# Edge scores of a graph attention layer: held scatters, a split slope and an adding gather

## The chip, the cores and the metric

The kernel runs on one core of a Trainium2 chip. The metric is the device time of one execution in microseconds, the median of the runs. Below, PE is TensorE, DVE is VectorE, ACT is ScalarE, POOL is GpSimd and SP is SyncE, which issues most DMAs here; ACTq and SPq are the instruction queues of ACT and SP.

## The reference

The program runs two layers over 1250 nodes with rows of 1024 numbers. Each layer is a graph part plus a linear attention, then a mixture of experts. The change touches the graph attention of the first layer:

```python
x = x * rsqrt(mean(x*x) + eps) * rms_w @ W_down      # 1250 x 256
xl = (x @ Wl).reshape(n, 4, 64);  xr = (x @ Wr).reshape(n, 4, 64)
msg = xl[src] + xr[dst]
act = where(msg > 0, msg, 0.2 * msg)
e = einsum('ehd,hd->eh', act, att)                   # a score for each edge and head
p = exp(e - segment_max(e, dst)[dst])
out = segment_sum(p / segment_sum(p, dst)[dst] * xl[src], dst) @ W_up
```

There are 20,000 edges in both directions plus one loop per node, 21,250 in all. The second layer also sums the rows of all sources of a node, so a table of how often an edge stands between two nodes is used twice.

## The kernel before

One core works through phases, one after the other; each phase is a block in which every engine has its own list of instructions, and all five meet at a barrier at its end. The core does not hold an edge list sorted by node. It writes the scores of all edges into a dense table `scores` in HBM (1250 x 1250 x 4 numbers, 25 MB), which is filled with -1e30 beforehand, and counts edges in a table `at`. The phases that matter:

- `norm_phase` (norm0, L116) normalizes `x`; ACT then issues 12 of the 40 tiles of the fill of `scores` (`Fill.issue`, L110, two DMAs each through `move_rows`, L35).
- `gat_project_phase` (L325): ACT issues the other 28 tiles first, then rounds the weights. PE computes `xl` and `xr`, which go to HBM, and DVE the scores of the loops (`loops`).
- `count_phase` (L548) sets up its tables (spans, node numbers), then for ten tiles of nodes DVE writes one-hot rows (`hot_d` L681, `hot_s` L683) that PE multiplies to counts (L755). ACT turns them round and SP stores them in `at`.
- `mix_phase` (mix0, L1063): linear attention in 8 slabs, bound to PE's matmuls. `output_phase` (out0, L1499) multiplies it with its weight.
- `gat_phase` (L768) reads `scores` and `at` tile by tile, takes the softmax and the weighted sum.

The edges ride along in three of them: they are cut in 85 batches of 250 edges (`EB` = 2 columns of 125). 18 batches are done in the count phase, 48 in mix0 (six per slab) and 19 in out0. For each batch POOL gathers the rows of `xl` and of `xr` with indirect DMAs (L478, two each), DVE computes the scores in `EdgeTurns.step` (L527: add L540, slope L541, times `att` L542, sum L543), and POOL scatters them into `scores` (L490, two). On POOL, `batch` (L483) waits for DVE's score of a batch, then issues scatter, gather, gather, scatter, gather, gather, where the gathers are for the batch two further on; each scatter waits until the one before it has landed (`s_sc`), since edges may repeat. The buffers have three slots (`RING`), and DVE copies the indices of each batch into a small tile (`columns`, L456). The diagonal is written by 11 small DMAs (L507) after the fill has landed.

Further on, `expert_phase` adds its rows into `x` with an indirect DMA that adds (L2136, 104 rows), and gathers with a plain one (L2123, 104 rows).

## Time and profile before

| what | value |
|---|---|
| median of 3 runs | 3541.19 us (3536.98 to 3546.23) |
| the profiled execution, own time | 3539.15 us |
| its span, first to last instruction | 3537.4 us |
| mean granted clock of PE | 0.871 |
| busy: PE, DVE, ACT, POOL | 77%, 46%, 25%, 26% |
| indirect DMAs issued by POOL for edges | 510 (170 scatters, 340 gathers) |

Times are microseconds from the span's start. An instruction of POOL that issues an indirect DMA is shown with the time in which POOL writes its descriptors; the transfer runs on behind it. In a line of a timeline the bracket tells how long the engine was idle before the instruction, and what ended that; "issue" means nothing that the profile can name. A wait for several semaphores is put down to the last one.

### The profile page before, as it was taken

The numbers are of one execution on the slowest core, as the hardware profiler recorded it, in microseconds if no ns is written. First come the engines' busy times: TensorE is split into PE (matmuls) and PEld (weight loads), VectorE is DVE, ScalarE is ACT, GpSimd is POOL, SyncE is SP. The second block draws the span as 40 slices with busy tenths as digits, with TensorE's granted clock in tenths as the row PEclk, the third lists the DMA queues.
The fourth block names the chain that finished last, engine by engine and source line by source line (L and its number), as shares of the span: only waits on it lengthen the run. The fifth ranks groups of instructions, "written<-read, shape, count | busy, mean of one in ns | idle before, by whom it ended". The sixth has DMA issues, their size and how long they took to land. (4 is left out here: it accounts for less than half of the span.)

```text
span 3537.4 us, 53669 instructions
## 1 busy us (share of the span) xinstructions
PE 2739.5 (77%) x19204; PEld 2520.8 (71%) x19204; DVE 1622.7 (46%) x3435; ACT 870.0 (25%) x1619; POOL 915.4 (26%) x790
## 2 busy tenths in 40 slices
PE   1267667887957659648995899899998979996458
PEld 1244457887847558637884899889997979996347
DVE  4078845554554359656554322223334422224445
ACT  3011023333211036313452101034442111101033
POOL 0036547677765612102221000000000000000054
PEclk6688888998978869857997899999998979998579
DMA  7722233333236398535874411111101553114064
GB/s 187 174 57 65 68 87 95 80 90 91 69 99 157 87 209 207 141 110 134 215 186 99 110 45 50 31 47 50 48 27 64 152 143 95 54 55 129 14 218 149
DMA packets 274009, 370.39 MB, mean 105 GB/s; under 512 B 89744, under 2 KB 218792, under 8 KB 272595
## 3 DMA queue, kind: packets, MB, share of 16 engines
q1 hardware_dynamic: 183797, 262.84, 26.4%
q0 software_dynamic: 63888, 80.33, 9.9%
q10 hardware_dynamic: 26160, 25.00, 3.0%
q8 instruction: 107, 1.75, 0.2%
q14 instruction: 57, 0.47, 0.0%
HBM read 279.45 MB, written 99.41 MB: 107 GB/s over the span
## 5 line engine op out<-in xcount | busy, mean ns | idle before, releaser
L299 PE MATMUL mix_bank<-mix_wkv_hi,layer_act_hi 128*125 128x256 f32 x1280 | 359.4, 281 | 0.0
L300 PE MATMUL mix_bank<-mix_wkv_lo,layer_act_hi 128*125 128x256 f32 x1280 | 359.3, 281 | 0.0
L301 PE MATMUL mix_bank<-mix_wkv_hi,layer_act_lo 128*125 128x256 f32 x1280 | 359.0, 280 | 0.0
L490 POOL DMA_INDIRECT scores<-edge_e,edge_now x170 | 216.9, 1276 | 249.9 <-issue 172.5
L300 PEld LDWEIGHTS mix_bank<-mix_wkv_lo,layer_act_hi 128*125 128x125 f32 x1280 | 237.7, 186 | 0.1
L301 PEld LDWEIGHTS mix_bank<-mix_wkv_hi,layer_act_lo 128*125 128x125 f32 x1280 | 237.7, 186 | 0.0
L299 PEld LDWEIGHTS mix_bank<-mix_wkv_hi,layer_act_hi 128*125 128x125 f32 x1280 | 237.3, 185 | 0.1
L478 POOL DMA_INDIRECT edge_gr<-xr,edge_now x170 | 217.1, 1277 | 51.8 <-issue 35.0
L478 POOL DMA_INDIRECT edge_gl<-xl,edge_now x170 | 213.8, 1258 | 59.7 <-issue 47.9
L299 PE MATMUL out_bank<-out_w_hi,layer_act_hi 128*125 128x256 f32 x640 | 190.7, 298 | 31.9 <-DVE out_w_lo L1598 22.8
L299 PE MATMUL sage_pz<-sage_wn_hi,layer_act_hi 128*125 128x256 f32 x640 | 181.7, 284 | 15.4 <-DVE sage_wn_lo L2364 15.4
L2484 PE MATMUL sage_pagg<-sage_z_hi,sage_cnt 125*125 125x256 f32 x800 | 192.8, 281 | 0.0
L2484 PE MATMUL sage_pagg<-sage_z_lo,sage_cnt 125*125 125x256 f32 x800 | 192.5, 281 | 0.0
L755 PE MATMUL count_pa<-count_hot_s,count_hot_d 125*125 125x416 bf16 (+1 forms) x624 | 147.8, 387 | 56.8 <-DVE count_hot_s L683 54.2
L300 PE MATMUL out_bank<-out_w_lo,layer_act_hi 128*125 128x256 f32 x640 | 185.7, 290 | 0.0
L301 PE MATMUL out_bank<-out_w_hi,layer_act_lo 128*125 128x256 f32 x640 | 185.4, 290 | 0.0
L300 PE MATMUL sage_pz<-sage_wn_lo,layer_act_hi 128*125 128x256 f32 x640 | 181.4, 284 | 0.0
L268 PE MATMUL norm_pt<-all_ident,norm_y 125*128 125x125 f32 x320 | 72.1, 417 | 141.2 <-DVE norm_y L196 141.2
L301 PE MATMUL sage_pz<-sage_wn_hi,layer_act_lo 128*125 128x256 f32 x640 | 181.2, 283 | 0.0
L299 PE MATMUL sage_pown<-sage_ws_hi,layer_act_hi 128*125 128x256 f32 x640 | 179.8, 281 | 0.0
L300 PE MATMUL sage_pown<-sage_ws_lo,layer_act_hi 128*125 128x256 f32 x640 | 179.5, 280 | 0.0
L301 PE MATMUL sage_pown<-sage_ws_hi,layer_act_lo 128*125 128x256 f32 x640 | 179.3, 280 | 0.0
(509 smaller groups left out, 7532.8 us busy)
## 6 DMA issues: line engine op xcount, KB each, us to landing
ffn_raw<-in_L_ffn_w_dram SPq DMA_DIRECT2D x16, 2048.0 KB
scores<-layer_hole ACTq DMA_DIRECT2D x40, 546.9 KB
gat_sc<-scores SPq DMA_DIRECT2D x10, 2187.5 KB
block_raw<-in_L_ffn_W_dram SPq DMA_DIRECT2D x16, 1024.0 KB
norm_x<-x SPq DMA_DIRECT2D x30, 448.0 KB
mix_raw<-in_L_mix_w_qkv_dram SPq DMA_DIRECT2D x24, 512.0 KB
sage_cnt<-at SPq DMA_DIRECT2D x20, 546.9 KB
out_part<-mixt SPq DMA_DIRECT2D x16, 625.0 KB
```

The costliest lines, as they stand in the source:

```text
L268: ins = pe.transpose(pt[h][:, k // 4, (k % 4) * R:(k % 4 + 1) * R], y[:, h, cols] if normalize else x[:, 2 * i + h, cols], ident[0:R, 0:R])
L299: pe.matmul(out, lhs[0], rhs[0], start=first, stop=False)
L300: pe.matmul(out, lhs[0], rhs[1], start=False, stop=False)
L301: return pe.matmul(out, lhs[1], rhs[0], start=False, stop=last)
L478: pool.indirect_dma_start(buf[:, slot, j, :], None, x, bass.IndirectOffsetOnAxis(ap=self.now[:, wide_slot, row, j:j + 1].bitcast(U32), axi ...
L490: pool.indirect_dma_start(self.scores, bass.IndirectOffsetOnAxis(ap=self.now[:, u % (2 * RING), 2, j:j + 1].bitcast(U32), axis=0), self.e[ ...
L755: ins = pe.matmul(pa[:, c, 0:n], hot_d[:, j, :], hot_s[:, j, o:o + n], start=False, stop=False)
L2484: ins = pe.matmul(pagg[u % 2][:, 0:SLAB], cnt[:, k, rows], z[s][:, k, :], start=(k, s) == (0, 0), stop=(k, s) == (T - 1, 1))
```

## The change

- `fill`: all 40 tiles of the fill are issued by SP: 12 at the end of its list in norm0, behind the loads of `x` and of the weights; 10 at the start of the projection; 18 at the start of the count phase.
- `Counts`: the setup of the count phase moves to the front of norm0, on SP, POOL, DVE and PE.
- The slope is split: leaky(m) = 0.8 max(m, 0) + 0.2 m. The part that is linear is computed as four more columns of `xl` and `xr` (`lin`, 8 columns from small matmuls), so their rows have 260 numbers (`ROW`). DVE's step is then max and times 0.8 `att` in one instruction, the sum, and an addition of 8 numbers per row.
- The row of `xr` is gathered with an addition in the DMA onto the row of `xl` (`add`). There are six slots; gathers run four batches ahead, adds three. The indices are read in place and `columns` goes.
- All scores stay in one tile `e`, and a batch is scattered later than it is computed (`written`, `LAG` = 8): none in the first eight iterations; then one batch per iteration with eight left open, two per iteration from iteration 19 to 25, and one behind from there on.
- `at` is laid out as (tile, row, tile, row), so that stores and loads of a tile are whole rows of 5000 bytes and not ten pieces of 500.

```diff
@@ Fill, norm_phase @@
-    def issue(self, act, n):
+    def issue(self, sp, n):
...
                 if load is not None:
                     load(sp)
+                if counts is not None:
+                    counts.fill.issue(sp, 12)
...
             @block.vector
             def _(dve):
+                if counts is not None:
+                    counts.vector(dve)
...
-                if fill is not None:
-                    for h in range(2):
-                        act.wait_ge(s_x[h], LANDED * T // 2)
-                    fill.issue(act, 12)
@@ gat_project_phase @@
             def _(sp):
+                fill.issue(sp, 10)
...
+                dve.tensor_tensor(slope[:, :, :].rearrange("p k (j n) -> p (k j) n", j=2),
+                                  wlr[:, :, :].rearrange("p k (j n) -> p (k j) n", j=2),
+                                  attb[:, :].unsqueeze(1).to_broadcast([P, 2 * KH, HID]), ALU.mult).then_inc(s_lin, 1)
...
             def _(act):
-                fill.issue(act, 28)
...
-                    if t >= 4:
-                        pe.wait_ge(s_xo, t - 3)
+                    if t >= 2:
+                        pe.wait_ge(s_xo, t - 1)
                     n = slice(t * R, (t + 1) * R)
+                    for k in range(KH):
+                        mm3(pe, plin[t % 2][:, 0:2 * HEADS], (d_hi[:, k, n], d_lo[:, k, n]), (lin_hi[:, k, :], lin_lo[:, k, :]),
+                            k == 0, k == KH - 1)
@@ Edges @@
-RING = 3
-AHEAD = 3
+RING = 6
+AHEAD = 4
+LAG = 8
...
+    def gather(self, pool, b):
+        slot = b % RING
+        if b >= RING:
+            pool.wait_ge(self.s_e, b - RING + 1)
+        for j in range(EB):
+            pool.indirect_dma_start(self.both[:, slot, j, :], None, self.xl, self.at(0, EB * b + j)) \
+                .then_inc(self.s_left[slot], 16)
+
+    def add(self, pool, b):
+        slot = b % RING
+        pool.wait_ge(self.s_left[slot], 16 * EB * (b // RING + 1))
+        for j in range(EB):
+            pool.indirect_dma_start(self.both[:, slot, j, :], None, self.xr, self.at(1, EB * b + j),
+                                    compute_op=ALU.add).then_inc(self.s_both[slot], 16)
+
+    def scatter(self, pool, b):
+        pool.wait_ge(self.s_e, b + 1)
+        for k in range(EB * b, EB * b + EB):
+            pool.wait_ge(self.s_sc, 16 * (T + 1) + 16 * k)
+            pool.indirect_dma_start(self.scores, self.at(2, k), self.e[:, k, :], None).then_inc(self.s_sc, 16)
...
+    def written(self, b):
+
+        return max(0, b + 1 - max(1, LAG - max(0, b - COUNT_BATCHES)))
 
     def gpsimd(self, pool, first, end):
...
+        for b in range(first, end):
+            if b + AHEAD < BATCHES:
+                self.gather(pool, b + AHEAD)
+            if b + AHEAD - 1 < BATCHES:
+                self.add(pool, b + AHEAD - 1)
+            for done in range(self.written(b - 1) if b else 0, self.written(b)):
+                if done == 0:
+                    self.diagonal(pool)
+                self.scatter(pool, done)
@@ EdgeTurns.step @@
-        link(dve.tensor_tensor(gl, gl, gr, ALU.add))
-        link(dve.scalar_tensor_tensor(gl, gl, 0.2, gl, ALU.mult, ALU.max))
-        link(dve.tensor_tensor(gl, gl, e.attb[:, :].unsqueeze(1).to_broadcast([R, EB, HID]), ALU.mult))
-        dve.tensor_reduce(e.e[:, slot, :, :], gl.rearrange("p t (a d) -> p t a d", a=HEADS), AX.X, ALU.add) \
-           .then_inc(e.s_e, 1)
+        dve.wait_ge(e.s_both[slot], 16 * EB * (turn + 1))
+        link(dve.scalar_tensor_tensor(x[:, :, 0:HID], x[:, :, 0:HID], 0.0,
+                                      e.attb[:, :].unsqueeze(1).to_broadcast([R, EB, HID]), ALU.max, ALU.mult))
+        link(dve.tensor_reduce(score, x[:, :, 0:HID].rearrange("p t (a d) -> p t a d", a=HEADS), AX.X, ALU.add))
+        dve.tensor_tensor(score, score, x[:, :, HID:], ALU.add).then_inc(e.s_e, 1)
@@ count_phase, gat_phase @@
             def _(sp):
-                for j, a in enumerate((src, dst)):
-                    sp.dma_start(rows_i[:, j, :], a.rearrange("(q e) -> q e", e=2 * R)).then_inc(s_rows, 16)
-                edges.sync(sp)
+                counts.fill.issue(sp, len(counts.fill.left))
                 for t in range(T):
                     sp.wait_ge(s_sb, t + 1)
-                    move_rows(sp, at.rearrange("b p d -> p b d")[:, :, t * R:(t + 1) * R], a_tr, s_st)
+                    move_rows(sp, at[t], a_tr, s_st)
```

How the change moves instructions shows best on POOL. Before, this is what POOL has for one batch in mix0's loop (L490 scatters, L478 gathers; names after "waits" in the loop are those of reused semaphores):

```order
L490 DMA scores<-edge_e,edge_now 1562500x4 [waits const_id]
L478 DMA edge_gl<-xl,edge_now 125x256
L478 DMA edge_gr<-xr,edge_now 125x256
L488 ISA
L490 DMA scores<-edge_e,edge_now 1562500x4 [waits const_id]
L478 DMA edge_gl<-xl,edge_now 125x256
L478 DMA edge_gr<-xr,edge_now 125x256
```

Between a scatter and the next one always stand two gathers. After the change, iterations 18 and 19 of POOL, the first two of mix0 (L507 gathers of `xl`, L514 adding gathers of `xr`, L521 scatters; `edge_sc` is the landing of earlier scatters):

```order
L507 DMA edge_both<-xl,edge_idx 125x260 [waits edge_e]
L507 DMA edge_both<-xl,edge_idx 125x260
L514 DMA edge_both<-xr,edge_idx 125x260 [waits edge_left3]
L514 DMA edge_both<-xr,edge_idx 125x260
L521 DMA scores<-edge_e,edge_idx 1562500x4 [waits edge_sc,edge_e]
L521 DMA scores<-edge_e,edge_idx 1562500x4 [waits edge_sc]
L507 DMA edge_both<-xl,edge_idx 125x260 [waits edge_e]
L507 DMA edge_both<-xl,edge_idx 125x260
L514 DMA edge_both<-xr,edge_idx 125x260 [waits edge_left4]
L514 DMA edge_both<-xr,edge_idx 125x260
L521 DMA scores<-edge_e,edge_idx 1562500x4 [waits edge_sc,edge_e]
L521 DMA scores<-edge_e,edge_idx 1562500x4 [waits edge_sc]
```

The second scatter of a batch now stands directly behind the first. Iterations 19 to 25 have a second batch of scatters behind the first, so four in a row, each waiting for the one before:

```order
L521 DMA scores<-edge_e,edge_idx 1562500x4 [waits edge_sc,edge_e]
L521 DMA scores<-edge_e,edge_idx 1562500x4 [waits edge_sc]
L521 DMA scores<-edge_e,edge_idx 1562500x4 [waits edge_sc,edge_e]
L521 DMA scores<-edge_e,edge_idx 1562500x4 [waits edge_sc]
L507 DMA edge_both<-xl,edge_idx 125x260 [waits edge_e]
```

The number of indirect DMAs is the same, 510; where they stand, and the kind of 170 of them, are new.

## Rows read from the trace of the kernel before

**Rows 1.** Count, mix0, out0, attention: length; busy PE, PEld, DVE, ACT, POOL; clock, DMA share
```profile
205.76:479.91 274.15, 174.26 (x796) 106.74 (x796) 209.35 (x551) 28.44 (x90) 156.76 (x134) 0.82 0.27 63
479.91:1011.57 531.66, 439.51 (x3078) 417.21 (x3078) 276.25 (x645) 161.42 (x399) 364.29 (x292) 0.91 0.33 85
1011.57:1243.94 232.37, 153.24 (x1082) 145.45 (x1082) 110.20 (x187) 20.64 (x27) 140.88 (x110) 0.80 0.49 119
1243.94:1470.00 226.06, 177.13 (x1326) 166.34 (x1326) 175.03 (x237) 116.66 (x68) 51.38 (x39) 0.88 0.86 194
```
**Rows 2.** Timeline of the first 152 us, ACT and its queue, then DVE and PE
```profile
50.76 24.25 ACTq L38 DMA_DIRECT2D scores<-layer_hole  x22
...
76.49 69.71 ACTq L38 DMA_DIRECT2D scores<-layer_hole  x56
146.24 1.91 ACT L385 ACTIVATE proj_wd_hi<-front_wd 128x2048 fp32r<-128x2048 f32 x1 [70.97 <-issue]
...
52.19 0.16 DVE L226 TENSOR_SCALAR front_rms<-norm_sumsq 125x10 f32<-125x10 f32 x1
...
150.53 0.71 PE L299 MATMUL proj_bank<-layer_act_hi,proj_wd_hi 128*128 128x418 f32 x1 [101.37 <-DVE proj_wd_lo L362]
```
**Rows 3.** Timeline of SP's queue: the last of the loads in norm0
```profile
28.38 0.37 SPq L322 DMA_DIRECT2D front_attb<-in_L_gnn_att_dram  x1
```
**Rows 4.** Groups of POOL in mix0 (480 to 1007): busy, mean ns, idle before
```profile
L478 POOL DMA_INDIRECT edge_gr<-xr,edge_now x96 | 122.2, 1273 | 29.3 <-issue 17.4 <-DMA scores<-edge_e,edge_now 11.9
L490 POOL DMA_INDIRECT scores<-edge_e,edge_now x96 | 121.0, 1261 | 104.1 <-issue 90.2 <-DMA scores<-edge_e,edge_now 12.1 <-DVE edge_now L457 1.5
L478 POOL DMA_INDIRECT edge_gl<-xl,edge_now x96 | 120.3, 1253 | 29.3 <-issue 25.6 <-DVE edge_e L543 3.7
```
**Rows 5.** Waits of PE and of DVE in mix0
```profile
PE mix_bank L299 <- DVE mix_sums_lo L1263: 62.3, 7, 9.6
DVE edge_gl L540 <- DMA edge_gr<-xr,edge_now: 69.8, 17, 5.7
```
**Rows 6.** Timeline of POOL: a scatter that had to wait, mix0; then its last scatters
```profile
593.86 1.22 POOL L490 DMA_INDIRECT scores<-edge_e,edge_now  x1 [0.30 <-issue]
...
599.67 1.22 POOL L490 DMA_INDIRECT scores<-edge_e,edge_now  x1 [1.55 <-DMA scores<-edge_e,edge_now]
...
1227.15 1.22 POOL L490 DMA_INDIRECT scores<-edge_e,edge_now  x1 [0.80 <-issue]
1230.66 1.42 POOL L490 DMA_INDIRECT scores<-edge_e,edge_now  x1 [2.29 <-DMA scores<-edge_e,edge_now]
```
**Rows 7.** POOL in the expert phase: adding DMAs against plain, groups; then a plain one
```profile
L2136 POOL DMA_INDIRECT x<-expert_out,ffn_chosen x24 | 38.7, 1611 | 174.8 <-DVE expert_out L2172 174.8
L2123 POOL DMA_INDIRECT expert_rows<-y,ffn_chosen x24 | 33.7, 1403 | 117.7 <-POOLq L68 82.0 <-DMA x<-expert_out,ffn_chosen 28.0 <-issue 5.2
...
1678.66 0.99 POOL L2123 DMA_INDIRECT expert_rows<-y,ffn_chosen  x1 [0.30 <-issue]
```
**Rows 8.** Groups of DVE in the count phase: an edge step's first two lines; index copies
```profile
L541 DVE SCALAR_TENSOR_TENSOR edge_gl<-edge_gl 125x512 f32<-125x512 f32 x18 | 12.5, 696 | 0.6
...
L540 DVE TENSOR_TENSOR edge_gl<-edge_gl,edge_gr 125x512 f32<-125x512 f32 x18 | 12.3, 685 | 9.8 <-DMA edge_gr<-xr,edge_now 9.8
L457 DVE COPY edge_now<-edge_idx 125x6 int32<-125x6 int32 x21 | 2.9, 147 | 0.0
```
**Rows 9.** Timeline of the count phase: first one-hot; last index copies; POOL at the end
```profile
219.92 0.45 DVE L681 TENSOR_SCALAR count_hot_d<-count_node,count_local 125x125 bf16<-125x125 f16 x1 [2.70 <-issue]
...
448.13 0.14 DVE L457 COPY edge_now<-edge_idx 125x6 int32<-125x6 int32 x1
...
473.64 1.21 POOL L478 DMA_INDIRECT edge_gr<-xr,edge_now  x1 [0.30 <-issue]
```
**Rows 10.** Waits of POOL and of DVE in out0
```profile
POOL scores L490 <- DMA scores<-edge_e,edge_now: 39.0, 14, 6.0
DVE edge_gl L540 <- DMA edge_gr<-xr,edge_now: 89.0, 14, 12.3
```

More of the change, by code:

```diff
@@ L143, in _ @@
             def _(sp):
+                if counts is not None:
+                    counts.load(sp)
                 if dst is not None:
@@ L165, in _ @@
                         sp.wait_ge(s_out[h], LANDED * (T // 2) + LANDED)
+            @block.gpsimd
+            def _(pool):
+                if counts is not None:
+                    counts.gpsimd(pool)
             @block.vector
             def _(dve):
+                if counts is not None:
+                    counts.vector(dve)
                 def statistics(i, link):
@@ L270, in pair @@
                         ins.then_inc(s_tr, 1)
+                if counts is not None:
+                    counts.tensor(pe)
                 pe.sem_inc(s_tr, 2)
@@ new lines, in scatter, with diagonal @@
+    def scatter(self, pool, b):
[3 more added lines that the diff above has]
+            pool.indirect_dma_start(self.scores, self.at(2, k), self.e[:, k, :], None).then_inc(self.s_sc, 16)
+    def diagonal(self, pool):
+        pool.wait_ge(self.fill.s_fill, self.fill.count)
+        flat = self.scores.rearrange("s h -> (s h)")
+        diag = flat[0:(N * N - 1) * HEADS].rearrange("(i x) -> i x", x=(N + 1) * HEADS)
+        for t in range(T):
+            n = min(R, N - 1 - t * R)
+            pool.dma_start(diag[t * R:t * R + n, 0:HEADS], self.loops[0:n, t, :]).then_inc(self.s_sc, 16)
+        pool.dma_start(self.scores[N * N - 1:N * N, :], self.loops[R - 1:R, T - 1, :]).then_inc(self.s_sc, 16)
@@ new lines, in written @@
+    def written(self, b):
+        return max(0, b + 1 - max(1, LAG - max(0, b - COUNT_BATCHES)))
+    def gpsimd(self, pool, first, end):
+        if first == 0:
+            pool.wait_ge(self.s_cell, 1)
+            for b in range(AHEAD):
+                self.gather(pool, b)
+            for b in range(AHEAD - 1):
+                self.add(pool, b)
+        for b in range(first, end):
[7 more added lines that the diff above has]
+                self.scatter(pool, done)
@@ L515, in gpsimd @@
         if end == BATCHES:
-            pool.wait_ge(self.s_sc, self.stored(end))
+            for done in range(self.written(end - 1), end):
+                self.scatter(pool, done)
+            pool.wait_ge(self.s_sc, 16 * (T + 1) + 16 * ET)
 class EdgeTurns:
@@ L630, in _ @@
                 link = Link(dve, s_link)
-                dve.wait_ge(s_iota, 3)
-                dve.tensor_copy(group[:, :, :], group_i[:, :, :])
-                dve.tensor_copy(node[:, :], node_i[:, :])
-                dve.tensor_copy(first[:, 0:1], tile_i[:, :])
-                dve.tensor_scalar(first[:, 1:2], tile_i[:, :], float(R), None, ALU.add)
-                dve.memset(ends[:, :, :, PAIRS:LAID], -1.0).then_inc(s_ends, 1)
-                dve.wait_ge(s_rows, 32)
-                ins = dve.tensor_copy(rows[:, :, :], rows_i[:, :, :])
@@ L664, in _ @@
-                dve.wait_ge(s_base, 1)
-                link(dve.tensor_copy(span[:, 3:4], pm[0:T, 1, 2 * PAIRS:2 * PAIRS + 1]))
-                dve.tensor_copy(span_i[:, :], span[:, :]).then_inc(s_span, 1)
-                dve.wait_ge(s_span, 1)
-                dve.wait_ge(s_ends, 2)
-                for t in range(T):
-                    dve.tensor_scalar(local[:, t, :, 0:LAID], ends[:, 1, :, 0:LAID], float(-R * t), None, ALU.add) \
-                       .then_inc(s_local, 1)
-                edges.vector(dve)
@@ L673, in _ @@
-                dve.wait_ge(s_local, T)
+                dve.wait_ge(counts.s_span, 1)
+                dve.wait_ge(counts.s_local, T)
                 todo = edges.turns(dve, 0)
```

358 lines of the change are left out of this document (185 added, 173 removed).

## Prediction

> **What bounds the kernel now.** I read the page's strips first (PE idle and DMA full early on; POOL busy to a third of the span), then busy time by stretch, then who waits for whom, then POOL's timeline. Three places matter.
>
> At the front, ACT stands in its own queue: 22 DMAs of the fill take 24.25 us to issue and 56 take 69.71 us, and only then does it round the weights on which PE's first matmul waits, 101.37 us in all [rows 2]. DVE's part of norm0 had ended at 52.2.
>
> In the count phase DVE is busy 209 of 274 us. In mix0 PE is busy 440 of 532 us [rows 1]; it loses 62.3 us to DVE, which loses 69.8 us to gathers [rows 5]. POOL is busy 364 us there, and each of its 288 instructions has 0.30 us of idle time before it that nothing explains [rows 4]: 364 + 86 = 450 of 532 us. So POOL has some 15% to spare in mix0. In out0, DVE waits 89.0 us for gathers and POOL 39.0 us for scatters to land [rows 10]; POOL's last scatter ends the phase, so POOL's list, read as a chain through the count phase, mix0 and out0, is what I cost.
>
> **The prices.** A plain gather costs POOL 1.26 + 0.30 = 1.56 us [rows 4], as does a scatter behind other work.
> A scatter directly behind a scatter starts 3.51 us after it in a quiet stretch (1227.15 to 1230.66), with 2.29 us of waiting for the landing; in mix0 one needed 5.81 us (593.86 to 599.67), while 90 of 96 came 4.6 us apart without waiting for it [rows 4, 6]. I take 3.6 us in the count phase and mix0 and 4.8 us in out0, where 14 scatters waited 39.0 us in spite of two gathers between them [rows 10]; the ends are 3.0 (a scatter landed just before a gather's end in 39 cases [rows 4]) and 5.8.
> An adding gather has no row. The nearest is the expert phase's adding scatter of 104 rows: 1.61 us, against 0.99 for a plain DMA of 104 rows [rows 7]. The difference, 0.63 us, I add: 2.19 us. Its lower end is 0 (adding cannot be cheaper to describe; the plain group's mean of 1403 ns, which holds stalls, would leave 0.21), its upper end 0.8 (the ratio 1.64 on 1.26).
>
> **The change, part by part.**
> 1. *Fill to SP.* ACT's stalls go. SP ends its loads at 28.8 us [rows 3], plus 1.9 us for five loads put in front, and issues 24 fill DMAs at about the 1.24 us each of ACT's 56, behind the loads still moving: to about 64. The setup in front of norm0 costs DVE about 8 us before the statistics, so DVE ends near 60 and SP is what is late next: norm0 ends at 66 and not 76.5. In the projection, rounding starts at once; PE's first matmul, 74.0 us after the second stall began [rows 2], comes 6.6 us after the phase's start: at 72.6 for 150.5, so 78 us earlier. SP's 20 further fill DMAs take 25 us and are covered by PE's 30 us of first matmuls before a row is stored. If that cover goes, the stores wait.
> 2. *Split slope, projection.* Some 60 small matmuls of one weight load each, at about 0.19 us, put PE at 2.5 us a tile where 1.95 us was the pace: +6 us. DVE's slope work (4 us) lies behind PE's four banks. The count phase starts at 134 and not 205.8: **-72**.
> 3. *Count phase.* The setup before the first one-hot (219.9, 14.1 us after the start [rows 9]) shrinks to 3.5. A tile without edge steps takes (228 - 16 x 3.05 - 9.8) / 10 = 17 us: from 219.9 to 448.1 there are 16 steps of four instructions of 0.69 us and a copy [rows 8, 9]. A step is now two of them and an addition, 1.65 us. DVE alone would need some 226 us. But POOL's iterations 6 and 7 are released at the end of the fourth tile, 82 us in, and from there it has 12 iterations: 12 x (2 x 1.56 + 2 x 2.19) = 90, ten pairs of scatters 10 x (1.56 + 3.6) = 52, the diagonal 6.4. With waits of some 4 us and the 5 us barrier, 240 us: POOL and DVE end nearly together. 274.2 to 240: **-34**. Mix0 starts at 374.
> 4. *Mix0.* POOL has 96 gathers, 96 adding gathers and, because eight batches were held back and are caught up here, 110 scatters. Of these 62 directly follow another (one in each of 41 iterations, three in each of seven). 96 x 1.56 + 96 x 2.19 + 48 x 1.56 + 62 x 3.6 = 150 + 210 + 75 + 223 = 658, with start and barrier 664 us. PE would need 532 - 62 - 10 = 460. The wait that goes (DVE's for gathers in three slots) comes back as the same wait behind POOL: six slots cover 20 us, not the 130 that POOL falls behind. 664 - 532: **+132**.
> 5. *Out0.* 30 gathers, 32 adding ones, 40 scatters of which 24 follow another: 47 + 70 + 25 + 115 = 257, with ends 265 us. 265 - 232: **+33**.
> 6. *Layout of `at`.* The attention phase's DMA share is 0.86 with DVE busy 175 of 226 us [rows 1]. Of some 48 MB moved there 6.25 MB are counts; I give whole rows a tenth of their 30 us: **-3**, between 0 and -15. Index copies leave DVE, which costs nothing now.
>
> Sum -72 - 34 + 132 + 33 - 3 = +56. The profiled execution took 3539.15 us, 2 us below the median of the runs: 3539 + 56 = **3595 us**.
>
> The Trainium skill's page "DMA: Bandwidth & Descriptors", section "Anatomy of one DMA — SWDGE (gpsimd) path", puts one such DMA at about 2.0 us plus bytes over 436 GB/s, and calls the writing of descriptors small. By that estimate a scatter behind a scatter would wait 2.0 us and not 3.6 or 4.8, the sum would be 182 us less, near 3413. This trace disagrees with it in rows 6, where 3.51 us pass in a quiet stretch.
>
> **The rivals.**
> - *Adding is free for POOL* (ends on the other side). If the adding gather's descriptors cost what plain ones do, because the extra 0.63 us belongs to rows of 4 KB or to a destination in HBM, 152 adding gathers on the chain (24, 96, 32) are 96 us cheaper: 3499 us. It decides below 0.37 us per add, 56 / 152. For it: the plain group's mean of 1403 ns is near 1611. Against it: POOL's time for plain ones doesn't follow the bytes (1.26 us for 16-byte scores as for 1 KB rows [rows 4]).
> - *Scatters land before they are missed.* If a scatter behind a scatter cost no more than its issue, 72 x 2.04 + 24 x 3.24 = 225 us go: 3370. Against it stands every pair in rows 6. The page above leans this way.
> - *Landing is slower behind adding gathers.* Each pair now follows two DMAs that read twice. At one more microsecond for the 96 exposed landings: 3691. For it: the 5.81 us [rows 6].
> - *In between*: a surcharge of 0.3 to 0.45 us, everything even: 3540 to 3550, no change to be seen.
>
> **Chances.** The forecast's own case 0.58, adding free 0.20, quick landing 0.06, slow landing 0.08, in between 0.08. The likeliest case's own range is 3550 to 3665 (surcharge 0.4 to 0.8, landing 3.3 to 4.1, front 10 us either way). The range given is 3495 to 3665, so that most of the free-adding case is in it, since cases of both signs hold most of the chance. A measurement of this kernel can tell about 0.3%, 11 us, from no change. Faster 0.26 (adding free and quick landing), same 0.08, slower 0.66.
>
> **What would show it.** Step 1: ACT rounds the weights about 2 us into the projection, PE's first matmul near 73, the count phase's start near 134. Step 3: that phase 240 us long, POOL with little idle at its end. Step 4: mix0 near 664 us, POOL's adding gathers at 1.9 us each, scatters waiting for scatters over 130 us in all, DVE waiting for the adding gathers, PE's clock and busy share lower. Step 5: POOL ends out0. I am wrong if adding gathers show 1.3 us, if the 62 exposed scatters start under 3 us behind their forerunners, or if mix0 is under 560 us with PE waiting for nothing of POOL's; or if SP's fill makes the projection's stores late.

## The result, and the profile after

The changed kernel takes 3689.2 us (median of 4 runs, 3686.9 to 3691.5) against 3540.1 us for the kernel before (3537.0 to 3546.2): a ratio of 1.041, with a 95% interval of 1.039 to 1.043. The prediction was 3595 us in a range of 3495 to 3665. The sign was right; the loss is 149 us where 56 were forecast, and the range was missed by 24 us. Medians and ratios below leave out one slow execution, of two_plain_lag5, which took 4286 us at a granted clock of 0.60.

The profiled execution took 3690.17 us, its span 3688.5 us; before it was 3539.15. The lengths of the stretches, by the first instruction of each phase in the timeline (the end of the table adds up to the whole difference of 151.0 us):

| stretch | before | after | difference | forecast |
|---|---|---|---|---|
| front (start of the count phase) | 205.7 | 126.8 | -78.9 | -72 |
| count phase | 274.2 | 268.0 | -6.2 | -34 |
| mix0 | 531.7 | 724.4 | +192.7 | +132 |
| out0 | 232.3 | 276.2 | +43.9 | +33 |
| attention and all behind | 2293.5 | 2293.1 | -0.4 | -3 |

Busy time by stretch, the counterpart of [rows 1]; columns as there (length; busy PE, PEld, DVE, ACT, POOL; clock; DMA share, GB/s):

```profile
127.00:394.80 267.80, 169.79 (x786) 102.63 (x786) 174.87 (x476) 28.50 (x90) 174.64 (x118) 0.82 0.53 108
394.80:1119.10 724.30, 468.66 (x3078) 439.59 (x3078) 219.12 (x549) 160.53 (x399) 446.95 (x305) 0.81 0.34 63
1119.10:1395.40 276.30, 151.81 (x1082) 144.01 (x1082) 86.34 (x152) 20.64 (x27) 156.25 (x106) 0.75 0.46 98
1395.40:1620.00 224.60, 175.98 (x1326) 164.71 (x1326) 172.10 (x239) 116.94 (x68) 51.52 (x39) 0.88 0.80 196
```

In mix0 DVE has 57 us less to do, as intended, but POOL has 83 more. PE needs 29 us more for the same 3078 matmuls: it is busy 65% of the stretch where it was 83%, and the granted clock is 0.81 where it was 0.91. What it stands for is one step away. The waits in mix0, the counterpart of [rows 5] (engine and tile, what it waited for, total us, times, longest):

```profile
DVE edge_both L576 <- DMA edge_both<-xr,edge_idx: 314.3, 36, 17.5
POOL scores L521 <- DMA scores<-edge_e,edge_idx: 198.3, 61, 6.6
PE mix_bank L311 <- DVE mix_sums_lo L1308: 81.1, 6, 19.0
PE mix_bank L1465 <- DVE mix_wkv_lo L1314: 73.2, 13, 14.5
```

PE waits for DVE (its sums and weights), DVE stands 314 us (69.8 before) for rows that the adding gathers bring, and POOL, which has to issue those, stands 198 us for scatters to land. POOL's groups in mix0, the counterpart of [rows 4] (count, busy us, mean ns, idle before):

```profile
L514 POOL DMA_INDIRECT edge_both<-xr,edge_idx x96 | 193.3, 2014 | 29.2 <-issue 29.2
L521 POOL DMA_INDIRECT scores<-edge_e,edge_idx x110 | 134.0, 1218 | 215.1 <-DMA scores<-edge_e,edge_idx 198.3 <-issue 14.3 <-DVE edge_e L579 2.6
L507 POOL DMA_INDIRECT edge_both<-xl,edge_idx x96 | 119.0, 1239 | 29.4 <-issue 22.7 <-DVE edge_e L579 6.7
```

Busy and idle add up to 193.3 + 134.0 + 119.0 + 29.2 + 215.1 + 29.4 = 720 of 724 us, and next to nothing of the idle time waits for another engine: POOL's list is the length of mix0. One iteration of it in the timeline, from a part without caught-up batches:

```profile
712.38 1.30 POOL L507 DMA_INDIRECT edge_both<-xl,edge_idx  x1 [0.30 <-DVE edge_e L579]
713.99 1.21 POOL L507 DMA_INDIRECT edge_both<-xl,edge_idx  x1 [0.30 <-issue]
715.50 2.01 POOL L514 DMA_INDIRECT edge_both<-xr,edge_idx  x1 [0.30 <-issue]
717.82 2.00 POOL L514 DMA_INDIRECT edge_both<-xr,edge_idx  x1 [0.30 <-issue]
720.12 1.24 POOL L521 DMA_INDIRECT scores<-edge_e,edge_idx  x1 [0.30 <-issue]
724.61 1.20 POOL L521 DMA_INDIRECT scores<-edge_e,edge_idx  x1 [3.26 <-DMA scores<-edge_e,edge_idx]
726.12 1.23 POOL L507 DMA_INDIRECT edge_both<-xl,edge_idx  x1 [0.30 <-DVE edge_e L579]
```

An adding gather takes 2.32 us from start to start, a plain one 1.52, and the second scatter starts 4.49 us after the first. Over all of mix0, from the starts in this timeline, the 48 scatters that directly follow a scatter behind adding gathers come 4.72 us behind it in the mean (median 4.51, shortest 4.23), the 14 that follow a second or third scatter 3.58. At the end of out0 POOL has scatters alone, and eight of them come 3.20 us apart in the mean:

```profile
1362.66 1.20 POOL L521 DMA_INDIRECT scores<-edge_e,edge_idx  x1 [3.11 <-DMA scores<-edge_e,edge_idx]
1366.11 1.18 POOL L521 DMA_INDIRECT scores<-edge_e,edge_idx  x1 [2.25 <-DMA scores<-edge_e,edge_idx]
1369.10 1.18 POOL L521 DMA_INDIRECT scores<-edge_e,edge_idx  x1 [1.81 <-DMA scores<-edge_e,edge_idx]
```

The front did what it should. From the timelines of SP's queue, ACT, PE and POOL, the counterpart of [rows 2, 3]:

```profile
36.16 51.02 SPq L38 DMA_DIRECT2D scores<-targets_hole  x44
65.22 1.91 ACT L415 ACTIVATE proj_wd_hi<-front_wd 128x2048 fp32r<-128x2048 f32 x1 [6.45 <-DVE front_wd L378]
69.50 0.72 PE L311 MATMUL proj_bank<-layer_act_hi,proj_wd_hi 128*128 128x418 f32 x1 [13.88 <-DVE proj_wd_lo L380]
126.79 69.25 SPq L38 DMA_DIRECT2D scores<-targets_hole  x36
```

PE's first matmul comes at 69.50 and not at 150.53. The start of the count phase is less settled than this one profile makes it look: nine of the runs below have the same front, fill and projection, and in them it lies between 125.2 and 135.5 us. The granted clock tells them apart. In all of them PE pauses for 1.28 us near 99 us, ahead of the second part of the projection. Here and in two_plain_lag1 the clock stayed at 1.00 (2.4 GHz) after it; in the other eight it stood at 0.5 (1.2 GHz) for 6.8 to 20.5 us. The stretch from 100 to 121 us, here and in two_plain_full_slope (columns as above):

```profile
100.00:121.00 21.00, 20.88 (x120) 17.43 (x120) 11.95 (x34) 7.61 (x18) 0.00 (x0) 1.00 0.34 100
100.00:121.00 21.00, 19.72 (x71) 16.57 (x70) 6.68 (x18) 4.75 (x11) 0.00 (x0) 0.59 0.17 50
```

PE is busy nearly all of it in both, and gets through 120 matmuls in one and 71 in the other. What decides whether the clock falls after this pause no run shows.

In the count phase DVE and POOL wait for each other (timelines of DVE and POOL; 216.28 begins iteration 6, 238.55 iteration 8):

```profile
177.05 0.66 DVE L742 TENSOR_SCALAR count_hot_d<-targets_node,targets_local 125x125 bf16<-125x125 f16 x1 [5.72 <-issue]
...
216.28 1.42 POOL L507 DMA_INDIRECT edge_both<-xl,edge_idx  x1 [7.08 <-DVE edge_e L579]
...
238.55 1.42 POOL L507 DMA_INDIRECT edge_both<-xl,edge_idx  x1 [7.07 <-DVE edge_e L579]
```

### The profile page after: what moved, and what is told of

It is laid out like the page before. It is cut to its first block and busy times, and to the rows that moved or that the text cites. A ratio compares the mean times of both kernels' runs of the same rounds, so it can differ in the third digit from the quotient of the medians.

```text
span 3688.5 us, 53108 instructions
## 1 busy us (share of the span) xinstructions
PE 2771.0 (75%) x19264; PEld 2546.9 (69%) x19264; DVE 1513.2 (41%) x3271; ACT 871.0 (24%) x1630; POOL 1034.3 (28%) x790
## 5 line engine op out<-in xcount | busy, mean ns | idle before, releaser
L514 POOL DMA_INDIRECT edge_both<-xr,edge_idx x170 | 344.2, 2025 | 54.9 <-issue 50.9
L521 POOL DMA_INDIRECT scores<-edge_e,edge_idx x170 | 210.5, 1238 | 350.9 <-DMA scores<-edge_e,edge_idx 324.5
L507 POOL DMA_INDIRECT edge_both<-xl,edge_idx x170 | 212.2, 1248 | 191.8 <-issue 165.4
L576 DVE SCALAR_TENSOR_TENSOR edge_both<-edge_both,edge_attb 125x512 f32<-125x512 f32 x85 | 58.5, 689 | 462.7 <-DMA edge_both<-xr,edge_idx 462.6
L2529 PE MATMUL sage_pagg<-sage_z_hi,sage_cnt 125*125 125x256 f32 x800 | 192.7, 281 | 0.0
```

Of the source, the lines that this page charges most:

```text
L507: pool.indirect_dma_start(self.both[:, slot, j, :], None, self.xl, self.at(0, EB * b + j)) \
L514: pool.indirect_dma_start(self.both[:, slot, j, :], None, self.xr, self.at(1, EB * b + j), compute_op=ALU.add).then_inc(self.s_both[slot], 16)
L521: pool.indirect_dma_start(self.scores, self.at(2, k), self.e[:, k, :], None).then_inc(self.s_sc, 16)
L576: link(dve.scalar_tensor_tensor(x[:, :, 0:HID], x[:, :, 0:HID], 0.0, e.attb[:, :].unsqueeze(1).to_broadcast([R, EB, HID]), ALU.max, ALU.mult))
L2529: ins = pe.matmul(pagg[u % 2][:, 0:SLAB], cnt[:, t, k, :], z[s][:, k, :], start=(k, s) == (0, 0), stop=(k, s) == (T - 1, 1))
```

## The experiments

Three explanations of POOL's long list stood against each other: the time that an adding gather takes to issue, the slower landing of what stands behind it, and the order, in which a scatter has nothing between it and the next. Each run names its own rivals A, B and C. This table holds all of them; the phases are read as above, from the first instruction of each in the profile. "Half clock" is how long the granted clock stood at half in the second part of the projection, from 95 us (before: 175 us) to PE's last matmul there, in us; the start of the count phase moves with it. The ratio is to runs of the kernel before on the same chip (medians 3547 to 3550 us, where 3540.1 was measured beside the change), so compare kernels by their ratios.

| run | median us | ratio (95%) | half clock | count starts | count | mix0 | out0 |
|---|---|---|---|---|---|---|---|
| before | | | 0 | 205.7 | 274.2 | 531.7 | 232.3 |
| the change | 3689.2 | 1.041 (1.039 to 1.043) | 0 | 126.8 | 268.0 | 724.4 | 276.2 |
| plain_add | 3507.8 (one run) | | 13.7 | 133.1 | 228.1 | 614.2 | 235.3 |
| adds_first | 3632.7 | 1.025 (1.022 to 1.028) | 13.7 | 134.0 | 278.4 | 671.8 | 258.7 |
| apart | 3608.1 | 1.018 (1.016 to 1.020) | 6.8 | 129.3 | 270.2 | 658.9 | 257.1 |
| apart2 | 3489.4 | 0.984 (0.982 to 0.985) | 20.5 | 134.9 | 233.3 | 598.4 | 234.2 |
| no_hold | 3700.1 | 1.043 (1.041 to 1.045) | 6.8 | 128.7 | 319.7 | 677.4 | 275.5 |
| front_only | 3464.1 | 0.978 (0.976 to 0.981) | 0 | 125.3 | 277.0 | 535.4 | 232.1 |
| two_plain_apart | 3411.0 | 0.963 (0.961 to 0.965) | 6.8 | 130.1 | 239.8 | 524.3 | 222.5 |
| two_plain_fill18 | 3424.1 | 0.965 (0.962 to 0.969) | 27.3 | 144.2 | 235.9 | 523.6 | 223.9 |
| two_plain_lag5 | 3393.0 | 0.956 (0.954 to 0.958) | 10.2 | 130.8 | 236.6 | 510.4 | 223.3 |
| two_plain_full_slope | 3405.6 | 0.959 (0.956 to 0.961) | 17.1 | 135.5 | 243.7 | 513.9 | 224.6 |
| two_plain_lag1 | 3382.2 | 0.953 (0.950 to 0.955) | 0 | 125.2 | 254.1 | 485.0 | 227.3 |

Everything behind out0 takes 2289 to 2298 us in all of them.

### plain_add: the addition taken out

```diff
-            pool.indirect_dma_start(self.both[:, slot, j, :], None, self.xr, self.at(1, EB * b + j),
-                                    compute_op=ALU.add).then_inc(self.s_both[slot], 16)
+            pool.indirect_dma_start(self.both[:, slot, j, :], None, self.xr, self.at(1, EB * b + j)) \
+                .then_inc(self.s_both[slot], 16)
```

> The changed kernel with the addition taken out of the second gather (the row of xr overwrites the row of xl; the addition of xl's rows is left out of the computation). Order and counts on POOL are the same. Theory A (an adding gather costs POOL 0.79 us more to issue, 2.31 instead of 1.52 us from start to start, and nothing else): about 150 of them lie on POOL's chain, so 3689 - 120 = 3570 us, mix0 648 us, and scatters behind the second gathers still start 4.5 to 4.7 us behind their forerunners. Theory B (the adding gathers also make the scatter behind them land late, because its packets stand behind theirs): on top of that the 72 exposed scatters behind adding gathers come at about 3.5 us instead of 4.7, another 85 us less: 3485 us, mix0 590 us. Rival C (neither; the order alone costs): no change beyond 20 us.

This kernel leaves the addition of the two rows out and so computes other scores; it issues the same 510 DMAs. Measured 3508 us, in one run, mix0 614.2. Its groups of POOL in mix0:

```profile
L521 POOL DMA_INDIRECT scores<-edge_e,edge_idx x110 | 132.6, 1206 | 182.7 <-DMA scores<-edge_e,edge_idx 168.1 <-issue 14.6
L514 POOL DMA_INDIRECT edge_both<-xr,edge_idx x96 | 116.6, 1214 | 29.3 <-issue 29.3
```

The second gather falls from 2014 to 1214 ns: 193.3 - 116.6 = 77 us of mix0's 110. The idle time ahead of scatters falls by 215.1 - 182.7 = 32 us: the 48 pairs come 4.01 us apart in the mean (median 3.59) and not 4.72 (median 4.51). So issue is the larger part and landing the smaller; B was right in kind, and its 85 us, put on 72 pairs, too large. But 614 is still 82 us above the 532 of before: the addition is not all.

### adds_first: which gathers stand right ahead of the scatters

```diff
-            if b + AHEAD < BATCHES:
-                self.gather(pool, b + AHEAD)
             if b + AHEAD - 1 < BATCHES:
                 self.add(pool, b + AHEAD - 1)
+            if b + AHEAD < BATCHES:
+                self.gather(pool, b + AHEAD)
```

> The changed kernel with one pair of calls swapped: in an iteration the two adding gathers come first, then the two plain gathers, then the scatters. Nothing else. Theory B (a scatter lands late because it stands right behind adding gathers in POOL's queue): behind plain gathers the second scatter of a pair starts 3.6 to 4.0 us after the first, as in plain_add, instead of 4.72: mix0 40 us shorter (685), total about 3689 - 60 = 3630 us. Theory A (the landing does not depend on what stands ahead): pairs stay at 4.7 us, mix0 724, total 3689 within 10. Rival C (the adding gathers' transfers are so long that two plain gathers, 3 us, don't clear them): pairs at 4.3 to 4.7 us, total 3670 to 3690.

Measured 3633 us. One iteration in the timeline:

```profile
709.94 2.05 POOL L514 DMA_INDIRECT edge_both<-xr,edge_idx  x1 [0.30 <-issue]
712.30 2.02 POOL L514 DMA_INDIRECT edge_both<-xr,edge_idx  x1 [0.30 <-issue]
714.62 1.24 POOL L507 DMA_INDIRECT edge_both<-xl,edge_idx  x1 [0.30 <-issue]
716.16 1.21 POOL L507 DMA_INDIRECT edge_both<-xl,edge_idx  x1 [0.30 <-issue]
717.68 1.21 POOL L521 DMA_INDIRECT scores<-edge_e,edge_idx  x1 [0.30 <-issue]
721.15 1.51 POOL L521 DMA_INDIRECT scores<-edge_e,edge_idx  x1 [2.26 <-DMA scores<-edge_e,edge_idx]
```

The same DMAs, and the pair is 3.47 us apart; the 48 pairs of mix0 have a mean of 3.67 (median 3.42), and mix0 is 53 us shorter, of which 48 x (4.72 - 3.67) = 50. B is shown: a scatter lands about 1.1 us later (0.9 in plain_add's medians) when adding gathers stand right ahead of it. The count phase lost 10 us, because adds now come too early after their own first gather and wait for it to land (49.5 us in the phase).

### apart and apart2: other issues between any two scatters

```diff
-            for done in range(self.written(b - 1) if b else 0, self.written(b)):
-                if done == 0:
-                    self.diagonal(pool)
-                self.scatter(pool, done)
...
+            out = (x for done in batches for x in self.scatter(pool, done))
+            for turn in (left, both) * EB:
+                next(turn, None)
+                if turn is both or len(batches) == 2:
+                    next(out, None)
...
```

`left` yields the plain gathers, `both` the adding ones, `out` the scatters, one at a time. Two gathers stand between two scatters, and one in the seven iterations that write two batches. This is apart2; apart had `(both, left)` and `turn is left`.

> The changed kernel with POOL's order in an iteration changed alone: add, gather, scatter, add, gather, scatter (with four scatters: add, scatter, gather, scatter, twice). Same DMAs, same result. Theory A (what costs is the landing of a scatter with nothing of POOL's between it and the next, 4.7 us from start to start where 1.5 is the issue): two other issues take 3.85 us, so a pair of scatters stands 5.4 us apart and waits for nothing; mix0 becomes 96 x 1.53 + 96 x 2.31 + 110 x 1.5 = 534 plus some 30 for the iterations with four: 565 to 575 us instead of 724, out0 about 210 instead of 276, the count phase 30 us shorter; total about 3440 us. Theory B (the landing only grows with what is queued, as every scatter now stands behind an adding gather): the waits come back in part, mix0 620 us or more, total 3530 or more. Theory C (something else, such as DVE or PE, bounds mix0 once POOL is faster): mix0 near 570 too but with waits of PE on something other than the edge steps.

> As the run apart, but within an iteration the order is gather, add, scatter, gather, add, scatter. In apart the second gather of a batch stood only one scatter ahead of the add that waits for its landing, and adds waited 61 us in the count phase and 35 (with the waits put down to scores, 88) in mix0. Here an add, a scatter and a gather stand between. Theory A (those waits were the flaw of my order, and an adding gather costs issue time above all): mix0 659 - 60 = 600 us, down to 565 if scatters wait for nothing, count phase 270 - 45 = 225, out0 235 to 245; total 3608 - 120 = 3490 us. Theory B (the landing behind adding gathers is what returns): scatters still wait 60 us or more in mix0, mix0 620 to 650, total 3530 to 3560. Either way mix0 stays above 532, since 96 x 2.31 + 96 x 1.53 + 110 x 1.5 is 534 on POOL with no wait at all.

Apart gave 3608 us and a mix0 of 659, far from A's 3440 and inside the bounds of its rival B (3530 or more, 620 or more). But most of the waiting stands in front of adds and not, as B had it, in front of scatters (68.4 us in mix0), by a flaw of my order: the adding gathers of apart in mix0, and in the count phase:

```profile
L516 POOL DMA_INDIRECT edge_both<-xr,edge_idx x96 | 197.3, 2056 | 104.0 <-DMA scores<-edge_e,edge_idx 52.3 <-DMA edge_both<-xl,edge_idx 35.4 <-issue 16.3
...
L516 POOL DMA_INDIRECT edge_both<-xr,edge_idx x42 | 87.4, 2080 | 70.7 <-DMA edge_both<-xl,edge_idx 60.9 <-issue 7.6 <-DMA scores<-edge_e,edge_idx 2.2
```

An add has nothing to wait for but the landing of its own first gather, which stood one scatter ahead of it. Apart2 exchanges the two kinds and nothing else:

```profile
L516 POOL DMA_INDIRECT edge_both<-xr,edge_idx x96 | 194.9, 2031 | 29.3 <-issue 29.3
L525 POOL DMA_INDIRECT scores<-edge_e,edge_idx x110 | 136.3, 1239 | 83.5 <-issue 38.7 <-DMA scores<-edge_e,edge_idx 37.0 <-DVE edge_e L591 7.8
```

3489 us, as A had it (3490), and mix0 598. The 215 us ahead of scatters have become 83.5. With the DMAs of the change, all adding gathers included, the order alone is worth 200 us, and the kernel is 1.6% faster than before (ratio 0.984, 0.982 to 0.985). And mix0 stays above 532, as POOL's issue time demands.

### front_only and two_plain_apart: the edges of before, or plain gathers with a better order

front_only keeps the front of the change and has `Edges`, `EdgeTurns` and the projection of before. two_plain_apart is apart2 without the adding gather, and so with three slots and gathers two batches ahead:

```diff
-RING = 6
-AHEAD = 4
+RING = 3
+AHEAD = 2
...
+        self.right = ph.sb("right", [R, RING, EB, ROW], F32)
...
-            pool.indirect_dma_start(self.both[:, slot, j, :], None, self.xr, self.at(1, EB * b + j),
-                                    compute_op=ALU.add).then_inc(self.s_both[slot], 16)
+            pool.indirect_dma_start(self.right[:, slot, j, :], None, self.xr, self.at(1, EB * b + j)).then_inc(self.s_both[slot], 16)
...
+        link(dve.tensor_tensor(x, x, e.right[:, slot, :, :], ALU.add))
```

> The kernel before with only the front of the change: fill issued by SP, the setup of the count phase in norm0, the layout of the count table. Edges, their order, their three slots, their plain gathers and the full slope are those of before. Theory A (the parts add up: front as in the changed kernel, a few us better without the small matmuls; count phase without its setup of 14 us but with the fill's end, near 200 us, ahead of the first scatter and the slots full until then): count phase starts at 121 and is 265 to 290 us long, mix0 532, out0 232, total 3465 to 3490 us. Rival B (the fill that still runs in the count phase costs nothing): count phase 260 us, total 3455. Rival C (the front's gain is given back by the fill's end): total within 15 us of 3540.

> The changed kernel with two plain gathers into two tiles of three slots each (the addition is DVE's again, 0.69 us more per step; gathers two batches ahead), the split slope, the held scatters, and on POOL the order gather, gather, scatter, gather, gather, scatter. Theory A (adding gathers and their order carried the whole loss): POOL's chain in mix0 is 192 x 1.53 + 110 x 1.5 + some 15 = 475 us, below PE's 460 to 490: mix0 480 to 510 us, out0 about 200, count phase 235 to 250; total 3540 - 78 - 30 - 35 - 30 = about 3365 us, range 3340 to 3400. Rival B (three slots are what mix0 and out0 lacked before, so DVE waits for gathers as it did): mix0 530, out0 230, total about 3430.

front_only came out at 3464, 83 us below the kernel before and at the lower end of A's range. The two profiles are 76.6 us apart, and the front, 80.4 us shorter, is all of that. The count phase is 277 us long as A had it, though 14 us of setup have left it; POOL stands there, ahead of the diagonal, until the fill has ended:

```profile
177.68 5.88 POOL L518 DMA_DIRECT2D scores<-layer_loops  x10 [39.35 <-DMA scores<-targets_hole]
```

two_plain_apart is at 3411, between its two expectations: mix0 gains 7 us and not 35, and DVE waits 89.5 us there for gathers, 69.8 before. B put that down to the three slots, but in the next two runs, with the same three slots and fewer scatters to catch up, the same wait is 64.2 and 42.0 us and mix0 510 and 485: most of the 28 us missed were the held scatters. Plain gathers with more slots were not tried. Against apart2 it is 78 us faster: with the same kind of order, and in spite of three slots instead of six, a plain gather and 0.69 us of DVE are cheaper than an adding gather.

### two_plain_lag5, two_plain_lag1, no_hold: how long scores are held

```diff
-LAG = 8
+LAG = 5
```

In two_plain_lag1 and no_hold it is `LAG = 1`; no_hold is the change itself with that one number.

> As two_plain_apart with scatters held five batches back instead of eight. There POOL waited 74 us in the count phase for DVE's scores, and six more scatters in mix0 and out0's chain are six fewer to catch up. Theory A (POOL's chain from mix0 on is what bounds): the count phase stays at 240 us, mix0 loses 6 x 2.5 = 15 us of 524, total 3395. Rival B (the diagonal then waits for the end of the fill and stops the gathers behind it): iteration 5 would be reached near 70 us into the count phase, the fill's last DMA lands about 60 us in, so no wait; if it lands later, POOL waits and the count phase grows by up to 20 us: 3415 to 3430. Rival C (mix0 is bound by PE and DVE, not by POOL): no change, 3411 within 8.

> As two_plain_lag5 with no scatters held back: from the second batch on, each batch is scattered one iteration later, so the diagonal and all behind it on POOL wait for the end of the fill in iteration 1. Theory A (holding scatters is worth the wait that front_only showed, 39.4 us of POOL behind the fill's end with DVE and PE standing 29 us behind it): the count phase grows from 236 to 260 to 275 us, mix0 and out0 lose the 8 scatters that were caught up there, 10 us; total 3395 + 15 to 30 = 3410 to 3425. Rival B (POOL had time to spare in the count phase, so only the chain behind it counts): total 3385, faster than with five held.

> The changed kernel with nothing held back: each batch is scattered one iteration behind, from the second iteration on; order within an iteration and adding gathers as in the change. Theory A (POOL's chain decides in the count phase too: it now stands from iteration 1 until the fill has landed, near 205 us on the trace's clock, and then has 17 iterations of 14.1 us and the diagonal's 9 before the phase can end): count phase 268 + 59 = 325 us, mix0 without its 14 caught-up scatters of 3.5 us 675, out0 276; total 3689 + 59 - 49 = 3699 us. Rival B (as two_plain_lag1 showed against two_plain_lag5, holding is not worth its catching up): total 3650 to 3675.

With the better order, five batches held gave 3393 us, A's number (3395). With none held I expected a loss, and was wrong: 3382, the fastest version, as its rival B had it (3385). POOL does wait for the fill (34.37 us):

```profile
179.17 6.38 POOL L532 DMA_DIRECT2D scores<-layer_loops  x10 [34.37 <-DMA scores<-targets_hole]
...
379.40:864.40 485.00, 434.62 (x3078) 414.73 (x3078) 250.27 (x597) 162.10 (x399) 361.87 (x292) 0.94 0.38 94
```

and the count phase is 17.5 us longer than with five held, but mix0 is 25 us shorter, at a clock of 0.94; out0 is 4 us longer. That leaves a gain of 4 us in the three phases that the hold touches; another 5.6 us lie ahead of them, where this run kept the full clock, and the intervals of the two ratios overlap. In the change itself no_hold came out as A had it (3700.1 for 3699), and its ratio, 1.043 (1.041 to 1.045), can't be told from the 1.041 of the change: 52 us more in the count phase against 47 less in mix0. What is clear of noise in both pairs is the shift. A held scatter is not saved; it moves behind the count phase, into the stretches whose length POOL sets, and costs there about what it spared.

### two_plain_full_slope and two_plain_fill18: two parts by themselves

```diff
 two_plain_full_slope
-        link(dve.scalar_tensor_tensor(x[:, :, 0:HID], x[:, :, 0:HID], 0.0,
-                                      e.attb[:, :].unsqueeze(1).to_broadcast([R, EB, HID]), ALU.max, ALU.mult))
+        link(dve.scalar_tensor_tensor(x[:, :, 0:HID], x[:, :, 0:HID], SLOPE, x[:, :, 0:HID], ALU.mult, ALU.max))
+        link(dve.tensor_tensor(x[:, :, 0:HID], x[:, :, 0:HID], e.attb[:, :].unsqueeze(1).to_broadcast([R, EB, HID]), ALU.mult))
...
-        dve.tensor_tensor(score, score, x[:, :, HID:], ALU.add).then_inc(e.s_e, 1)
...
 two_plain_fill18
-                fill.issue(sp, 10)
+                fill.issue(sp, 18)
```

> As two_plain_lag5 with the split slope undone in the edge steps: add, slope, times att, sum, four instructions of 0.69 us instead of three and one of 0.17; the linear columns are still computed and gathered, but not used. DVE gets 85 x 0.52 = 44 us more work. Theory A (DVE's length decides in the count phase alone, where POOL waits 61 us for scores): 18 x 0.52 = 9 us there, a few more in mix0 where PE waits 46 us for DVE: total 3405 to 3415. Rival B (DVE is covered everywhere by POOL's chain): 3395 within 6. Rival C (PE's waits for DVE in mix0 grow by all of 25 us): total 3430.

> As two_plain_apart, with 18 tiles of the fill issued at the start of the projection and 10 in the count phase instead of 10 and 18. Theory A (the fill in the count phase slows its first tiles: DVE's idle time at the start of tiles that nothing explains is 33 us there against 22 in the kernel before, and count stores wait behind it): the fill ends 20 us earlier, 10 to 15 us of those come back, and SP is free at 107 us when the first store of xl would be issued at 103: total 3395 to 3405. Rival B (the stores of xl and xr come late behind the fill, in SP's list or in the DMA queues): the count phase starts 5 to 20 us later, total 3415 to 3430. Rival C: both even out, 3411 within 8.

two_plain_full_slope is two_plain_lag5 with the full slope, two_plain_fill18 is two_plain_apart with more of the fill in the projection. The full slope came out at 3405.6 against 3393.0, ratios of 0.959 and 0.956 whose intervals overlap; the phases say more: 7 us in the count phase and 3.5 in mix0, A's numbers, and nearly 5 ahead of them that belong to the clock. So the split takes 44 us off DVE and some 10 off the program.

Moving more of the fill into the projection lost 13 us: the count phase gained 4, and its start came 14 us later. SP reaches its first store at 109.85 instead of 104.60, and its third store of `xl` at 118.96 instead of 111.59. In between ACT stands for 10.12 us for which the profile names nothing; what comes next is its third tile, and in the program that waits until the first tile's stores have left the buffer. PE stands for 5.71 us, and then the granted clock is at half from 118.2 to 135.3. That is B, with the clock on top: half clock takes 27.3 us here and 6.8 there. The fill in the count phase was not what made its first tiles slow, or only by these 4 us.

## Why the prediction was right and wrong

**Front (steps 1 and 2), -72 forecast, -78.9 measured: right, and a little lucky.** SP issued its DMAs at 51.02 / 44 = 1.16 us each, and nothing had to wait for them. PE's first matmul came 3 us earlier than worked out, and from there to the count phase it took 57.3 us where before it were 55.1: the small matmuls and what belongs to them cost 2 us and not 6. That holds for a projection at full clock, as in this profile. In adds_first, with the same front, the clock stood at half for 13.7 us, and the count phase began at 134.0, the forecast's own figure. The forecast had no term for the clock.

**Count phase (step 3), -34 forecast, -6.2 measured: the release was mis-timed, and the pairs were too cheap.** I let POOL run freely from iteration 6 on. But iteration 8 waits for a score of DVE's fifth tile just as iteration 6 waits for the fourth's; it was to start at 82 + 15 = 97 us into the phase and started at 238.55 - 126.8 = 111.8. The tiles took 22 to 23 us with their two steps, not 17 + 3.3: the one-hot instructions of L742 had a mean of 372 ns where it was 321, and at the starts of tiles DVE was idle for 35.9 us that nothing explains, 22.3 before. That is 15 us. The other 13 are the ten pairs of scatters, 66 us instead of 52, and the diagonal, 8 instead of 6, and adding gathers that were 3 us dearer, less some 4 us of waits that I had allowed for.

**Mix0 (step 4), +132 forecast, +192.7 measured: the right mechanism, one term too small.** POOL's list is the length of mix0, DVE waits for adding gathers, PE for DVE, and the granted clock is lower. The terms, from start to start:

| term of step 4 | forecast | measured |
|---|---|---|
| 96 adding gathers | 2.19 each, 210 | 2.32 each, 223 |
| 48 scatters behind a scatter that follows adding gathers | 3.6 each, 173 | 4.72 each, 226.5 |
| 14 behind a second or third scatter | 3.6 each, 50 | 3.58 each, 50 |
| gathers and other scatters | 1.56 each, 225 | 219 |

Nine tenths of the 60 us missed are the second line. I had taken the landing from a quiet stretch with scatters alone, 3.51 us, and that is what the third line shows; but three quarters of the exposed scatters stand behind two adding gathers. The rival "landing is slower behind adding gathers" had this mechanism, and at one more microsecond its time, 3691, within 2 us of the result, which is luck: its price was put on all 96 exposed landings, and only the 73 directly behind adding gathers have it, while other terms missed the other way. It got a chance of 0.08, with nothing for it but the 5.81 us of [rows 6], and the trace before had no adding gather ahead of a scatter to read it from.

**The price of adding.** 2.19 was worked out from a difference of 0.63 us between DMAs of 104 rows [rows 7], put unscaled on one of 125 rows. The expert phase's 1.61 us are 15.5 ns a row, the adding gather's 2.01 are 16.1; the plain ones are 9.5 and 9.8. Scaled by rows I would have had 1.94 + 0.30 = 2.24 of the 2.32. The rival "adding is free" is excluded: 2014 ns against 1214 in plain_add. Two sums beside it were wrong: 56 / 152 = 0.37 us is what an add would have to be cheaper than forecast for the change to even out, so that rival decides below a surcharge of 0.63 - 0.37 = 0.26 us and not 0.37; and a surcharge of 0.3 to 0.45 us gives 3545 to 3568 us, not 3540 to 3550.

**Out0 (step 5), +33 forecast, +43.9 measured.** Its 24 exposed scatters took 120 us where 115 were forecast: 16 at 5.90 and 8 at 3.20, so 4.8 for all hid two prices. The adding gathers were 5 us dearer, the ends 3.

**Layout of `at` (step 6), -3 forecast, -0.4 measured:** nothing that can be told. The DMA share of the attention phase fell from 0.86 to 0.80, and its length did not follow.

**Quick landing.** The estimate from the Trainium skill's page "DMA: Bandwidth & Descriptors", section "Anatomy of one DMA — SWDGE (gpsimd) path", by which a scatter would wait 2.0 us, is not what these runs show: the shortest distance of two scatters in a row was 2.78 us, the mean of the 22 with only scatters ahead 3.44, and behind adding gathers 5.02 over all 73. About 1.2 us of each is POOL's own issue of the scatter ahead; counted from the end of that issue the 22 come 2.25 us later in the mean and those behind adding gathers 3.8. So with only scatters ahead the 2.0 us are not far off as a wait behind the issue; behind adding gathers they are.

**What the forecast did not ask** was whether the order was the fault. It took the pairs as part of the change's price. They are the larger part of it: apart2 has every DMA of the change and is 200 us faster.

The step that failed, in one line: step 4's price of a scatter directly behind a scatter, 3.6 us where 4.72 was measured behind adding gathers (54 of the 94 us missed), with the same price and the release of iteration 8 in step 3 (28).

## What to carry to other kernels

When an engine's list is read as a chain of DMAs of which each waits for the one before, the order is a price of its own: put two independent issues between two dependent ones, and look where each of those two gets its own input from, as apart shows. Take the landing time of a DMA from a place where the same things stand ahead of it in its queue. And work that is held back to spare a wait in one stretch can only gain if the stretch that takes it up has room; with plain gathers and five batches held it went from a phase in which POOL waited 61 us for scores to one in which it waited 21.

## What the runs showed of the hardware

- An indirect DMA that adds takes GpSimd 2.03 to 2.07 us to issue for 125 rows, a plain one 1.22 to 1.28 (means over the 170 of a kind, by run). That is 16 ns a row against 10, and the expert phase's DMAs of 104 rows, 1.61 and 0.99 us [rows 7], lie at the same two figures, though their rows are longer. So at these two sizes the time goes by rows.
- The additions change the number of packets on POOL's queue and not the bytes. The page's line of the queue in the change, then in plain_add (packets, MB, share of 16 engines):

```profile
q0 software_dynamic: 112848, 81.19, 12.4%
```
```profile
q0 software_dynamic: 63888, 81.01, 10.2%
```

  170 adding gathers bring 48960 more packets, 288 each: in the trace's packets an adding gather moves its rows one by one (1040 bytes), a plain one mostly four at a time (4160 bytes).
- The packets also show where the later landing comes from. Over the 48 pairs of mix0, the first scatter's own 16 packets begin 2.04 us after POOL starts to issue it, and 1.95 in adds_first: no difference. They end after 3.82 us against 2.90, and the last packet with gathered rows ends after 3.79 against 2.52. So 0.9 of the 1.05 us lie in the time in which the scatter's packets run beside the rows of the adding gathers ahead. In both the next scatter starts 0.8 to 0.9 us after the last of these packets.
- In two_plain_fill18 SP was done with 60 DMAs of the fill at 109.85, 5 us behind the time at which two_plain_apart issued its first store; yet its third store of `xl` came 7 us later than there and the phase ended 14 us later. ACT and then PE stood in between, and the clock fell. What is queued goes on costing after the issuing engine is free.
- From its first matmul to its last the same projection took PE 51.3 us when the clock stayed full after the pause, and 60.2 us with 17.1 us at half clock (two_plain_lag1 and two_plain_full_slope). A few microseconds at the start of a later phase can be the clock and not the change.
